# Four cross-attention layers on one core: the two blocks made one, a wide unit's value matmuls cut from ten to eight, and the wide step written in another order

## What is computed

```python
# layers 0 and 2 ("wide"): 16 heads of 64
logits = einsum('bhqd,bhkd->bhqk', x @ Wq, ctx @ Wk) * 64**-0.5 + col_bias
x = softmax(logits) @ (ctx @ Wv) -> (B, HW, 1024) @ Wo + bo + x
# layers 1 and 3 ("narrow"): 16 query heads of 32, 4 key/value heads
xn = rmsnorm(x) * norm_w
x = x + (softmax(xn @ wq @ k / sqrt(32)) @ v) @ wo
```

## Time and profile before

| | us |
|---|---|
| median of 3 runs | 2129.08 (2128.84 to 2129.55) |
| the profiled execution, its own time | 2129.63 |
| its span, first to last instruction | 2127.6 |
| PE busy | 2080.0 (98%) |
| DVE busy | 1353.4 (64%) |
| ACT busy | 925.6 (44%) |
| POOL busy | 621.3 (29%) |

### The profile page before, as it was taken

How to read it: one execution, slowest core, us unless ns; L and a number is a source line. 1 busy time by engine, 2 the same in 40 slices (tenths; PEclk the granted TensorE clock), 3 DMA queues, 4 the chain that set the end, 5 groups by cost and what they waited for, 6 DMA issues and landing times.

```text
span 2127.6 us, 31233 instructions
## 1 busy us (share of the span) xinstructions
PE 2080.0 (98%) x11674; PEld 1794.6 (84%) x11674; DVE 1353.4 (64%) x2344; ACT 925.6 (44%) x1750; POOL 621.3 (29%) x454
## 2 busy tenths in 40 slices
PE   8999989999999998999999999999999989999998
PEld 8999978888888887788888888888888877888886
DVE  5333355755576556688888675557655765888885
ACT  3222244533354335455555453335433543555552
POOL 0000042212221245454444331222122433444431
PEclk9999989999999999999999999999999999999999
DMA  7877842222222222343333332212221222233322
GB/s 202 187 158 157 176 119 72 71 62 71 58 65 63 75 62 71 86 110 101 86 94 93 102 94 63 72 56 65 63 75 52 70 72 80 69 93 88 87 71 81
DMA packets 260727, 191.00 MB, mean 90 GB/s; under 512 B 195842, under 2 KB 198306, under 8 KB 258018
## 3 DMA queue, kind: packets, MB, share of 16 engines
q1 hardware_dynamic: 260578, 189.02, 35.1%
HBM read 132.66 MB, written 56.26 MB: 89 GB/s over the span
## 4 chain that ended last, share of the span: by engine, by line
PE 80%; DVE 4%; ACT 1%; issue 1%; POOL 1%; SPq 0%; DMA 0%; DVEq 0%; POOLq 0%; ACTq 0%
PE acc_bank L812 12%; PE q_bank L773 8%; PE acc_bank L234 8%; PE q_bank L777 8%; PE q_bank L775 8%; PE acc_bank L236 8%; PE acc_bank L235 8%; PE t_bank L795 7%; PE s_bank L736 2%; PE s_bank L234 2%; PE s_bank L733 2%; PE s_bank L739 2%; PE s_bank L236 2%; PE s_bank L235 2%; DVE prob L1068 1%
## 5 line engine op out<-in xcount | busy, mean ns | idle before, releaser
L1205 POOL TENSOR_TENSOR prob<-prob,rinv 128x1232 f32<-128x1232 f32 x128 | 288.3, 2252 | 1096.5 <-DVE rinv L1100 1096.5
L812 PE MATMUL acc_bank<-pT_s,vals_s 128*128 128x512 f32 x1152 | 370.2, 417 | 0.0
L1064 DVE TENSOR_REDUCE mx<-s_bank 128x4 f32<-128x308 f32 x512 | 241.0, 471 | 195.1 <-PE s_bank L739 125.8
L977 ACT ACTIVATE q_s<-q_bank 128x512 fp32r<-128x512 f32 x192 | 114.7, 598 | 538.9 <-PE q_bank L777 534.3
L773 PE MATMUL q_bank<-x_s,w_s 128*128 128x512 f32 x768 | 321.1, 418 | 4.0 <-POOL w_s L1198 4.0
L777 PE MATMUL q_bank<-x_s,w_s 128*128 128x512 f32 x768 | 315.0, 410 | 0.0
L775 PE MATMUL q_bank<-x_s,w_s 128*128 128x512 f32 x768 | 314.0, 409 | 0.0
L234 PE MATMUL acc_bank<-o_s,w_s 128*128 128x512 f32 x752 | 304.5, 405 | 1.4 <-DVE o_s L1091 1.3
L236 PE MATMUL acc_bank<-o_s,w_s 128*128 128x512 f32 x752 | 298.1, 396 | 0.0
L235 PE MATMUL acc_bank<-o_s,w_s 128*128 128x512 f32 x752 | 297.5, 396 | 0.0
L968 ACT ACTIVATE prob<-prob,rstd 128x308 f32<-128x308 f32 x256 | 140.5, 552 | 288.1 <-DVE prob L1068 270.0
(11 more groups left out here) (104 smaller groups left out, 3950.6 us busy)
## 6 DMA issues: line engine op xcount, KB each, us to landing
stream<-x_back SPq DMA_DIRECT2D x128, 256.0 KB, 2.6
x_front<-stream SPq DMA_DIRECT2D x96, 256.0 KB, 3.5
x_back<-stream SPq DMA_DIRECT2D x96, 256.0 KB, 3.9
kvw_raw<-kvw SPq DMA_DIRECT2D x17, 1024.0 KB, 9.1
k_scr<-k_out SPq DMA_DIRECT2D x36, 308.0 KB, 9.6
keys_s<-k_scr SPq DMA_DIRECT2D x128, 77.0 KB, 2.5
v_scr<-v_out SPq DMA_DIRECT2D x8, 1024.0 KB
x_back<-x_in SPq DMA_DIRECT2D x32, 256.0 KB, 4.2
```

Of the source, the lines that this page charges most:

```text
L812: mm = pe.matmul(out, w, pT_s[:, part], start=i == mine[0] and part == 2 * n and w is v[0], stop=i == mine[-1] and w is terms[-1][0] and p ...
L1064: dve.tensor_reduce(top, scored, AX_X, ALU.max).then_inc(s_max, 1)
L1205: pool.tensor_tensor(view, view, rinv[:, slot].unsqueeze(2).broadcast_to([P, TILES * GH, CTX]), ALU.mult).then_inc(p_norm, 1)
```

## The change

- **One block.** The context's instructions and the attention's stand in one block, engine by engine, one behind the other. Waits on semaphores stand where the barrier was: PE waits for the drained key banks (`k_lo`) and the last split weights (`late_lo`), DVE and SP for the stored keys, SP, POOL and ACT for the stored values. The first loads of the attention (`begin`) are issued inside the context's rounds 3 to 6, into buffers of their own.
- **Eight value matmuls.** `rest` holds the rest columns twice, so T2 has 128 rows. ACT copies the high part of each pair of heads twice (one instruction for each m), DVE the low part (two instructions of 32 partitions), POOL clears the partitions above; the values' rest block is laid three times (high, low, high), with 10 DMAs a wide unit in place of 8. The rest block then takes one product: V is 4 a chunk, not 5.
- **Another order of the wide step.** PE: S of tiles 0 and 1 in a row, 12 Q, S of tiles 2 and 3 in a row, 12 Q, 4 V, T0, 4 V, T1, T2. ACT and DVE follow. On DVE `denominators` stands ahead of the second query chunk, the values and the transposes, and the low part of T2 (`rest_t(u, TWICE)`) is moved into the next step, behind tile 1.
- Narrow steps keep their order.

The core of the diff:

```diff
-            row = REST_A * m + P - (PAIR - REST_A)
-            pieces += [(2 * m, 0, CTX, first, 0, 2), (2 * m + 1, 0, P - CTX, first, CTX, 2),
-                       (2 * m + 1, P - CTX, CTX, rest, row, 2), (2 * m + 1, P - CTX, CTX, rest, 64 + row, 1)]
+            row = P - (PAIR - REST_A)
+            pieces += [(2 * m, 0, CTX, first, 0, (0, 2)), (2 * m + 1, 0, P - CTX, first, CTX, (0, 2))]
+            pieces += [(2 * m + 1, P - CTX, CTX, rest, REST_A * slot + row, parts)
+                       for slot, parts in enumerate(((0, 1), (1, 2), (0, 1)))]
...
+    def rest_later(self, u):
+
+        return kind(u).name == "A" and u + 2 < NU and kind(u + 2).name == "A"
...
+            if 3 <= j < 7:
+                begin(j - 3)
...
+            def begin(part):
+                if part == 0:
+                    sp.wait_ge(context.k_stored, context.wide_keys)
+                    sp.wait_ge(context.v_stored, context.wide_vals)
+                    sp.wait_ge(keys_zeroed, 2)
+                    load_keys(0)
+                    load_keys(1)
+                    load_weights(0)
+                    load_weights(1)
+                elif part < 3:
+                    sp.wait_ge(vals_zeroed, 2)
+                    load_vals(part - 1)
+                else:
+                    for k in range(RING):
+                        load_front(1, k)
+                    for m in range(XC):
+                        load_back(0, m)
+
+            context.sync(sp, begin)
             for s in range(STEPS):
+                if s == 0:
+                    sp.wait_ge(context.k_stored, context.all_keys)
+                    sp.wait_ge(context.v_stored, context.all_vals)
...
-                        rows, p = 64, rest[:, t] if a else prob[:, u % 2, t, SC - REST_B:SC]
+                        rows, p = (P, rest[:, t]) if a else (64, prob[:, u % 2, t, SC - REST_B:SC])
...
-                        terms = [(v[0], 2 * n), (v[1], 2 * n)] if n == TWICE else \
-                            [(v[0], 2 * n), (v[0], 2 * n + 1), (v[1], 2 * n)]
+                        terms = [(v[0], 2 * n), (v[0], 2 * n + 1), (v[1], 2 * n)]
+                        if n == TWICE:
+                            terms = [(v[0], 2 * n + m)] if kind(u).name == "A" else [(v[0], 2 * n), (v[1], 2 * n)]
...
+            context.tensor(pe)
+            pe.wait_ge(context.k_lo, context.all_drained)
+            pe.wait_ge(context.late_lo, 3)
...
-                    beside(scores(s, 0), q, half)
-                    beside(scores(s, 1), q, half)
-                    beside(scores(s, 2), v, 5)
+                    run(scores(s, 0), 6)
+                    run(scores(s, 1), 6)
+                    run(q, half)
+                    run(scores(s, 2), 6)
+                    run(scores(s, 3), 6)
+                    run(q, half)
+                    run(v, 4)
                     turned(0)
-                    beside(scores(s, 3), v, 5)
+                    run(v, 4)
                     turned(1)
                     turned(2)
...
+                if n == TWICE and kind(u).name == "A":
+                    for m in range(2):
+                        e = act.activation(pT_s[0:64, 2 * n + m], t_bank[(3 * u + n) % 2][64 * m:64 * m + 64, :],
+                                           ACT.Copy)
+                    e.then_inc(t_hi, 1)
+                    return
...
                 if s < NU and kind(s).name == "A":
-                    next(q, None)
                     bias(s, 2)
-                    next(q, None)
                     bias(s, 3)
                     exps(s, 0)
+                    next(q, None)
+                    bias(s + 1, 0)
+                    bias(s + 1, 1)
+                    exps(s, 1)
+                    next(q, None)
+                    weights()
                     if pv == 2:
                         split_o(s - 2, 0)
                     turned(0)
-                    bias(s + 1, 0)
-                    weights()
                     if pv:
                         split_o(s - 2, pv - 1)
                     turned(1)
-                    bias(s + 1, 1)
                     turned(2)
-                    exps(s, 1)
                     fresh_x()
...
+                if n == TWICE and kind(u).name == "A":
+                    for m in range(2):
+                        e = dve.tensor_tensor(pT_s[64:64 + REST_A, 2 * n + m],
+                                              t_bank[(3 * u + n) % 2][64 * m:64 * m + REST_A, :],
+                                              pT_s[0:REST_A, 2 * n + m].bitcast(F32), ALU.subtract)
+                    e.then_inc(t_lo, 1)
+                elif n == TWICE:
...
                     tile_scores(s, 0)
+                    tile_scores(s, 1)
+                    if s >= 2 and plan.rest_later(s - 2):
+                        rest_t(s - 2, TWICE)
                     for gb, m in plan.late(s - 1):
                         add_result(gb, m)
                     next(q, None)
-                    tile_scores(s, 1)
+                    tile_scores(s, 2)
+                    tile_scores(s, 3)
+                    denominators(s)
                     next(q, None)
-                    tile_scores(s, 2)
                     if pv == 2:
                         rest_o(s - 2, 0)
                     turned(0)
-                    tile_scores(s, 3)
-                    turned(1)
                     if pv:
                         rest_o(s - 2, pv - 1)
-                    turned(2)
-                    denominators(s)
+                    turned(1)
+                    if s >= 1 and not plan.rest_later(s - 1):
+                        rest_t(s - 1, TWICE)
                     for gb, m in plan.projections(s):
...
+                    twice = rest[:, :, :].rearrange("q t (w d n) -> q t w d n", w=2, d=2)
                     ends = prob[:, slot].rearrange("q t (w n) -> q t w n", w=2)[:, :, :, PAIR - REST_A:PAIR]
-                    pool.tensor_copy(rest[:, :, :].rearrange("q t (w n) -> q t w n", w=2), ends)\
-                        .then_inc(p_gathered, 1)
+                    for copy in range(2):
+                        ins = pool.tensor_copy(twice[:, :, :, copy], ends)
+                    ins.then_inc(p_gathered, 1)
```

More of the change, by code:

```diff
@@ L15 @@
+from collections import namedtuple
 from contextlib import ExitStack
@@ L263, in context_block, with sb, sem @@
     assert NJ == B + 1
+    early = ExitStack()
+    def sb(name, shape, dt):
+        return early.enter_context(nc.sbuf_tensor(name, shape, dt))
+    def sem(name):
+        return ctx.enter_context(nc.semaphore(name))
+    ctx_raw = sb("ctx_raw", [P, KC, ROWS], F32)
+    ctx_s = sb("ctx_s", [P, 2, KC, ROWS], F32R)
+    w_raw = sb("kvw_raw", [P, 2, PART], F32)
+    k_out = sb("k_out", [P, 2, 2, ROWS], F32R)
+    v_out = sb("v_out", [P, len(VROWS), 2, BLK], F32R)
+    banks = [early.enter_context(nc.psum_tensor(f"ctx_bank{i}", [P, 512], F32)) for i in range(8)]
@@ L662, in load_vals @@
                 vals = vals_s[:, slot].bitcast(F32)
-                for h, t0, t1, blk, row, parts in kind(u).pieces:
-                    src = (v_scr[4 * p + g, b, t0:t1, 0:parts, w * h:w * h + w] if kind(u).name == "A"
-                           else v1_scr[p, b, t0:t1, 0:parts, w * g:w * g + w])
+                for h, t0, t1, blk, row, (first, last) in kind(u).pieces:
+                    src = (v_scr[4 * p + g, b, t0:t1, first:last, w * h:w * h + w] if kind(u).name == "A"
+                           else v1_scr[p, b, t0:t1, first:last, w * g:w * g + w])
                     col = w * h % P
-                    sp.dma_start(vals[row:row + t1 - t0, blk, 0:parts, col:col + w], src)\
+                    sp.dma_start(vals[row:row + t1 - t0, blk, 0:last - first, col:col + w], src)\
                       .then_inc(vals_loaded[slot], 16)
@@ L864, in run @@
                     next(work, None)
-            def beside(small, large, n):
-                for i in range(6):
-                    next(small, None)
-                    run(large, n * (i + 1) // 6 - n * i // 6)
+            context.tensor(pe)
+            pe.wait_ge(context.k_lo, context.all_drained)
+            pe.wait_ge(context.late_lo, 3)
             for i in range(2):
```

570 lines of the change are left out of this document (280 added, 290 removed).

## The result

The changed kernel takes 2164.01 us (median of 4 runs, 2162.58 to 2165.72), the kernel before 2129.32 (4 runs beside it, 2128.84 to 2130.33): 1.0163 times as long, interval 1.0145 to 1.0180. The prediction was 2160, 4 us less. The profiled execution spans 2163.9 us, 36.3 more than before.

A forecast was written before the change was run, and what follows sets the result against it. It took the loop of PE waiting at T2 for DVE's list to bound the wide step: 2129.6 + 42.3 - 9.2 - 1.9 = 2160.8, on the median 2160 us. Forecast range 2143 to 2177; 8 in 10, 2104 to 2184.

The forecast's parts named there:

- The walk: DVE's new list in a wide step, link by link to T2: step 12.6 against 11.87 us, 58 steps +42.3 us.
- The two upper bounds: Links in DVE's chain to T2: exponential behind its bias 0.43 us at most, reciprocal 0.25 at most.
- The two pieces of 32 partitions: Older T2's low part on DVE, behind tile 1's subtraction: each costed like 64 or 128 partitions, both over by 4.0 us.
- The 0.9 us of idle time: DVE idle before the first query chunk of a wide step, 0.9 us, hiding the price of the two T2 pieces.
- The seam: Context to attention: first score matmul at 267.7, 10.4 us earlier, less 1.2 for a query-chunk wait: -9.2 us.
- The wait for the second query chunk: At the seam, the second half of a score tile waits for DVE's second query chunk, taking 1.2 us back.
- Narrow steps: Steps 32, 33, 96 and 97 carry the last wide values: 8 x 0.2325 = -1.9 us.
- SP and POOL: SP's ten value loads in place of eight and POOL's second copy of the rest columns cost nothing.
- Steps 1, 31, 64, 65 and 95: Steps that mix both forms, taken as 0, -3 to +3 us.
- The clock, third rival: Clock falls after the 58 waits of 1.2 us: 2256 us, or 2184 after one in four; chance 12%.
- PE alone bounds, second rival: PE's saved matmuls come off whole: 2129 - 29.8 - 9.2 = 2090 us; chance 5%.
- T0's own path, first rival: DVE less late, only T0's path through ACT and DVE binds: T2 at 11.3, step 11.67, 2106 us; chance 12%.

The follow-up runs named there:

- e1_t0_first: Changed kernel with one swap on DVE: T0's low part ahead of the first value chunk's; 2132.41 us, 1.0014 of the kernel before.
- e5_t2_next_step: Changed kernel with T2 moved behind the next step's first scores on PE in plain wide steps, ACT's order adapted; 2094.47 us, 0.9835 of the kernel before.
- e3_order_alone: Kernel before (two blocks, ten value matmuls) with only the new wide-step order on PE, ACT and DVE; 2169.91 us, 1.0195 of the kernel before.
- e2_old_order: Changed kernel (one block, eight value matmuls) with the old wide-step order on PE, ACT and DVE; 2098.68 us, 0.9859 of the kernel before.
- e4_one_block: Kernel before with only the barrier gone and first loads issued early (old order, ten value matmuls); 2114.89 us, 0.9936 of the kernel before.
- e6_entry: Changed kernel with DVE's row sums behind the second query chunk and T0's low part in steps 0 and 1 alone; 2163.28 us, 1.0161 of before.
- e8_entry_weights: Changed kernel, steps 0 and 1 only: DVE's sums behind T0's low part, ACT's weight pieces behind the transposes; 2160.30 us, 1.0145 of before.
- e10_sums_behind_t0: Changed kernel with DVE's row sums and reciprocal moved behind T0's low part in all wide steps; 2147.42 us, 1.0087 of the kernel before.

## Why the prediction was right, point by point

- **The walk.** From the first query chunk on every point was within 0.15 us (8.64 against 8.62 at `sums`, 12.57 against 12.6 for the step). The 58 steps cost 41.3 us (19.4 + 18.8 + 2.4 + 0.7) where 42.3 were forecast. `e1_t0_first` showed that its last link binds, `e5_t2_next_step` that without it a step falls to PE's own list. Of this 41.3 some 1.7 are not the walk's but step 2's slow clock (2.4 against 0.7). The two upper bounds (0.43 and 0.25 us) measured 0.36 and 0.17; the other links were off by up to 0.07 either way, and together they leave the 0.1 us by which the walk was long.
- **The two pieces of 32 partitions.** I took the whole price; each costs 0.685 us, as much as 64 or 128 partitions. They were over at 4.29 and not at 4.0, as tile 1's subtraction came 0.14 late and they start half a microsecond behind it. The 0.9 us of idle time covered that too: 0.72 were left.
- **The seam.** -9.9 and -0.3 in step 0, against -9.2 in all: two errors of opposite sign. The first score matmul came at 268.25 and not at 267.7, as the context itself ended 0.6 later in this execution (262.47); the other runs with one block have it between 267.5 and 268.3. The wait for the second query chunk was 1.12 us (forecast 1.2), but step 0's own waits of 0.41 and 0.83 in the old order went, so that step 0 became 0.3 shorter and not 1.2 longer.
- **Narrow steps.** -1.9, as forecast, but by luck: the 8 x 0.2325 are not what these steps show. With ten value matmuls and the new order (`e3_order_alone`) they took 4.5 us less than before, with eight and the old order (`e2_old_order`) 5.0 more. What they take depends on how late DVE and ACT come out of the wide steps.
- **SP and POOL.** Nothing, as forecast: no wait of PE in the attention is put down to a load of keys or values or to POOL.
- **Steps 1, 31, 64, 65 and 95: the mis-sized term.** I took 0, -3 to +3; they took 7.4, of which 3.9 are step 1, where DVE's late chunk lies open. I had the walk in hand and did not redo it with PE's shorter list. The other 3.5 are 1.4, 0.6, 1.5 and 0.0. In steps 31 and 95 PE has only the narrow unit's queries, is at T2 early and waits 4.1 us for the same T0, the clock at 0.71 and then 0.50 behind that in step 31. But before, PE waited in both steps too (2.0 us for weights, 1.0 for a bias), and step 95, with a lower clock, took the 15.06 that it takes now; step 31, with the same waits and the clock at 1.00, took 13.46 (before, windows of step 31 and of step 95):

```profile
804.00:807.00 3.00, 2.79 (x16) 2.44 (x17) 2.83 (x5) 0.44 (x1) 0.79 (x2) 1.00 0.52 117
1725.00:1728.00 3.00, 3.00 (x13) 2.52 (x12) 2.30 (x4) 0.04 (x1) 1.02 (x1) 0.62 0.55 163
```

  `e4_one_block`, in the old order, has them at 15.06 and 15.04. So the 1.4 of step 31 can't be put down to the new order. In step 65 ACT waited 1.3 us for a piece of weights that stands ahead of T0 in the new order:

```profile
1225.46 0.63 ACT L1042 ACTIVATE w_s<-stage 128x512 fp32r<-128x512 f32 x1 [1.32 <-DMA stage<-woA]
```

  In `e6_entry` and `e8_entry_weights`, whose code is the same there, it did not, and step 65 took 17.6 in place of 18.8. What the order itself costs at these edges is thus step 1 and some 0.8 us of steps 64 and 65.
- **The clock, third rival.** It did not fall behind the waits of 1.00 us, and did behind those of 2.23 and 4.1. The rival's mechanism shows in this kernel at the edges alone.
- **PE alone bounds, second rival.** Its 2090 was wrong for this order. The Trainium skill, "Perfetto Trace Analysis", section "Identifying the Most-Contended Engine", says to optimize first the engine with the highest occupancy. That is PE in both kernels, at 98% and 95%. For TensorE the same passage has the headroom judged by MFU (the share of the peak arithmetic rate) and the busy share of weight loads, which is 84% and 82% here, and it promises no gain; the 2090 was my sum. The trace shows why it failed: the wait that ends each step is in none of these shares. Once T2 is out of the loop the time comes near that sum: `e5_t2_next_step` is at 2094.47.
- **T0's own path, first rival.** DVE was late as walked, so it did not come to this. The path itself was sized right, as the steps behind the projections in `e10_sums_behind_t0` show.

In span the forecast was +31.2 us and the result +36.3: 7.4 more in the edge steps, 1.0 less at the seam, 1.0 less in the 58 steps, 0.3 less in the rest. The mechanism and its size were right; that the whole came within 4 us is helped by errors that partly cancel.

## What to carry to other kernels

Read from the window of one step how far each engine is from idle, then walk the new order once round the loop; a share of busy time can't tell that an order costs 0.7 us a step and swallows the 0.47 saved besides. Where an instruction waits for a bank at the end of a list, look first whether it can stand a microsecond later on its own engine: here that gave 69 us (with ACT's new order), and reordering the engine it waits for gave 32 and 17. And redo the walk for the steps in which the pipeline fills or drains, since there the work that covers a late link is missing.
